# A mixture-of-depths stage in a megakernel: two batches in the row halves, one rank pass, three pairs in flight

## What is computed

```python
h = h + _L2_ffn_ref(_layernorm(h, axis=-1), ...)

def _L2_ffn_ref(x, attention_mask, wr, br, w1, b1, w2, b2):
    k = max(1, int(0.5 * s))
    kk = k - 1 if k > 1 else 1
    weights = (jnp.einsum('bsd,do->bso', x, wr) + br)[..., 0]
    _, idx = jax.lax.top_k(weights, k)
    sel_idx = idx[:, :kk]
    sel = jnp.take_along_axis(x, sel_idx[:, :, None], axis=1)
    hid = jax.nn.gelu(jnp.einsum('bkd,dh->bkh', sel, w1) + b1)
    y = jnp.einsum('bkh,hd->bkd', hid, w2) + b2
    y = y * jnp.take_along_axis(weights, sel_idx, axis=1)[..., None]
    processed = jnp.zeros_like(x).at[batch_idx, sel_idx].set(y)
    return processed + x
```

## Time and profile before

| | |
|---|---|
| median of three runs | 6034.58 us |
| the profiled execution's own time | 5997.16 us |
| its span, first to last instruction | 5995.3 us |
| mean granted TensorE clock over it (1 is 2.4 GHz) | 0.818 |
| busy: TensorE matmul | 5041.0 us (84%) |
| busy: TensorE weight loads | 3453.3 us (58%) |
| busy: VectorE | 3205.9 us (53%) |
| busy: ScalarE | 2330.2 us (39%) |
| busy: GpSimd | 1898.2 us (32%) |

### The profile page before, as it was taken

One profiled execution on the slowest core, in us unless ns is written; L12 is line 12 of the kernel. 1 busy time (PEld: TensorE's weight loads), 2 busy tenths in 40 slices (PEclk: granted clock), 3 DMA queues, 4 the chain that ended last, 5 costly groups with the idle time before them and its releaser, 6 DMA issues. The chain is left out here.

```text
span 5995.3 us, 119454 instructions
## 1 busy us (share of the span) xinstructions
PE 5041.0 (84%) x34045; PEld 3453.3 (58%) x34045; DVE 3205.9 (53%) x9147; ACT 2330.2 (39%) x5857; POOL 1898.2 (32%) x2148
## 2 busy tenths in 40 slices
PE   4419998576677999979997668879999999979999
PEld 4416665355465666656665655545666666646665
DVE  1145553344353466634443446657777777745554
ACT  3313333000011233334442321116777777745555
POOL 0002222111153344422223740004444444433333
PEclk9997776555596699979997555558999999989999
DMA  0010011111121011133331111110000000023332
GB/s 9 7 36 19 21 22 14 33 39 40 39 56 34 19 26 26 25 69 75 81 78 41 42 36 26 27 33 8 10 10 8 10 10 10 9 44 68 75 74 60
DMA packets 522888, 205.69 MB, mean 34 GB/s; under 512 B 491164, under 2 KB 513804, under 8 KB 522636
## 3 DMA queue, kind: packets, MB, share of 16 engines
q1 hardware_dynamic: 522764, 204.15, 15.4%
HBM read 158.15 MB, written 45.91 MB: 34 GB/s over the span
## 5 line engine op out<-in xcount | busy, mean ns | idle before, releaser
L3083 POOL TENSOR_TENSOR att_P<-att_P,att_rden 125x498 f32<-125x498 f32 x512 | 520.8, 1018 | 633.2 <-DVE att_rden L3354 633.2
L3270 ACT ACTIVATE att_P<-att_pS,att_nb 125x249 f32<-125x249 f32 x1024 | 472.7, 476 | 0.3 <-DVE att_nb L3362 0.3
L2474 DVE TENSOR_TENSOR moe_hT<-moe_silu,moe_pH 128x498 f32<-128x498 f32 x384 | 258.9, 674 | 324.3 <-ACT moe_silu L2460 324.3
L3691 ACT ACTIVATE sw_hT<-sw_pH,sw_b 128x498 f32<-128x498 f32 x512 | 318.4, 673 | 242.7 <-PE sw_pH L3645 242.7
L3186 PEld LDWEIGHTS att_pP<-att_ident,att_P 124*125 124x125 f32 (+1 forms) x2048 | 262.5, 187 | 181.0 <-issue 181.0
L3186 PE MATMUL att_pP<-att_ident,att_P 124*125 124x124 f32 (+1 forms) x2048 | 352.5, 294 | 3.8 <-POOL att_P L3083 2.4
L3362 DVE TENSOR_REDUCE att_nb<-att_pS 125x2 f32<-125x498 f32 x512 | 323.0, 668 | 58.1 <-PE att_pS L3174 56.4
L3277 ACT ACTIVATE att_PTr<-att_pP 125x498 f32<-125x498 f32 x512 | 304.9, 596 | 97.7 <-PE att_pP L3186 91.9
L2460 ACT ACTIVATE moe_silu<-moe_pH 128x498 f32<-128x498 f32 x384 | 225.4, 587 | 284.2 <-PE moe_pH L2417 198.4
L1021 PE MATMUL att_pS<-att_kT,att_qT 16*125 16x249 f32 x1024 | 304.7, 482 | 2.1 <-ACT att_kT L1127 1.3
L586 POOL TENSOR_TENSOR att_norm_centered<-att_F,att_norm_sum 125x256 f32<-125x256 f32 (+1 forms) x128 | 85.2, 666 | 662.1 <-DVE att_norm_sum L581 661.8
(11 more groups left out here) (452 smaller groups left out, 12166.2 us busy)
## 6 DMA issues: line engine op xcount, KB each, us to landing
moe_share<-mixing SPq DMA_DIRECT2D x64, 498.0 KB
sw_share<-mixing SPq DMA_DIRECT2D x64, 498.0 KB
att_F<-h_stream SPq DMA_DIRECT2D x192, 62.5 KB
att_X<-h_stream SPq DMA_DIRECT2D x192, 62.5 KB
ffn_w<-in_w1b SPq DMA_DIRECT2D x128, 32.5 KB
ffn_w<-in_L_ffn_W SPq DMA_DIRECT2D x128, 32.0 KB
h_stream<-att_H SPq DMA_DIRECT2D x64, 62.5 KB
ffn_F<-h_stream SPq DMA_DIRECT2D x64, 62.5 KB
```

The costliest lines, as they stand in the source:

```text
L3083: g.tensor_tensor(own, own, bc(rden[:, j % 2, c, :], T), ALU.mult).then_inc(*scaled.one())
L3270: ins = a.activation(P[:, r, c, t, :], pS[:, 2 * r + c, t * T:(t + 1) * T], ACT.Exp, bias=nb[:, r, c, t:t + 1], accum_out=den[:, r, c, t:t ...
L3691: a.activation(hT[:, k % 4, :, :], pH[:, place, :, 0:T], ACT.Relu, bias=b1[:, k:k + 1]).then_inc(*hid_ready.one())
```

## The change

Only `stage_depths2` and its constants change. The new stage is written with `HalfNorm` and `waves`, in three parts (`pre`, `proj`, `main`) of four steps each.

- Both batches of a pair are transposed together, so xT is 128 rows (64 channels of each batch) x 249. Gate and hidden products run once per batch in the row half of that batch (64 rows), the w2 product once per batch and half of the hidden channels onto the column half (64 output rows of pY) of that batch. pY has channels on its rows and is transposed back by two transposes into pT.
- The biases come through ScalarE's bias operand (br for W, b1 for the gelu, b2 for yT) instead of a row of ones.
- A token's own weight comes by four one-row transposes of W on TensorE and a copy of 125x4. The rank of a group is one VectorE instruction: (W - own weight) > tie, summed, where tie is 0 or, for earlier tokens, the negative of the smallest normal number.
- Centering, squares and scaling of the norm move from VectorE and ScalarE to GpSimd, and so do the two closing additions: base = X + xn, and H1 = res + base. The copy to xT moves to ScalarE. VectorE's gate is one instruction.
- SyncE's order is that of `streamed`: F is loaded four pairs ahead, X two pairs ahead, each behind the store in program order.

```diff
+    STEPS, WAVES, ROUNDS = 4, 4, 6
+        norm = HalfNorm(st, bodies=WAVES)
...
+                streamed(sp, ahead, keep, store, 4)
...
             def _(g):
...
+                def pre(n, u, step):
+                    if step == 0:
+                        g.wait_ge(*xn_ready.before(n))
+                        norm.center(g, n, g4(Fi[:, u, :, :, :]))
+                        norm.square(g, n)
+                    if step == 2:
+                        norm.power(g, n)
+                    if step == 3:
+                        if since(n, 2):
+                            g.wait_ge(*xT_done.after(n - 2))
+                            g.wait_ge(*base_ready.after(n - 2))
+                        norm.scale(g, n, g4(xn[:, u, :, :, :])).then_inc(*xn_ready.one())
+                def main(n, u, step):
+                    if step == 1:
+                        g.wait_ge(*kept.after(n, u))
+                        g.wait_ge(*xn_ready.after(n))
+                        g.wait_ge(*h_ready.before(n))
+                        g.tensor_tensor(base[:, :, :], g4(X[:, u, :, :, :]), g4(xn[:, u, :, :, :]), ALU.add).then_inc(
+                            *base_ready.one())
+                    if step == 3:
+                        g.wait_ge(*res_ready.after(n))
+                        g.wait_ge(*base_ready.after(n))
+                        g.wait_ge(*stored.lagging(n, u))
+                        g.tensor_tensor(g4(H1[:, u, :, :, :]), res[:, :, :], base[:, :, :], ALU.add).then_inc(
+                            *h_ready.one())
+                waves(g, (pre, lambda n, u, step: None, main), STEPS)
...
             def _(pe):
...
+                def proj(n, u, step):
                     if step == 0:
+                        pe.wait_ge(*xn_ready.after(n))
+                        pe.wait_ge(*xT_ready.before(n))
+                        for t in range(2):
+                            ins = pe.transpose(pX[:, t * OFF:t * OFF + ROWS[t]],
+                                               xn[0:ROWS[t], u, t, :, :].rearrange("p b c -> p (b c)"),
+                                               ident[0:ROWS[t], 0:ROWS[t]])
+                    if step == 1:
+                        pe.wait_ge(*xT_ready.after(n))
+                        pe.wait_ge(*w_ready.before(n))
+                        pe.wait_ge(*hid_ready.before(n))
                         for b in range(2):
+                            r = slice(b * C, (b + 1) * C)
+                            ins = pe.matmul(pW[:, b, 0:T], wr[r, :], xT[r, :], start=True, stop=True)
+                        ins.then_inc(*w_done.one())
+                        for k in range(2):
+                            for b in range(2):
+                                r = slice(b * C, (b + 1) * C)
+                                ins = pe.matmul(pH[:, b, k * T:(k + 1) * T], w1[r, k * 128:(k + 1) * 128], xT[r, :],
+                                                start=True, stop=True)
+                def main(n, u, step):
+                    if step == 0:
+                        pe.wait_ge(*w_ready.after(n))
+                        pe.wait_ge(*n_ready.before(n))
+                        for t in range(2):
+                            for b in range(2):
+                                g = 2 * t + b
+                                ins = pe.transpose(pN[:, g:g + 1], W[0:1, u, b, t * OFF:t * OFF + PT],
+                                                   ident[0:1, 0:1])
+                    if step == 1:
+                        pe.wait_ge(*hid_ready.after(n))
+                        pe.wait_ge(*yT_ready.before(n))
+                        for k in range(2):
+                            for b in range(2):
+                                ins = pe.matmul(pY[b * C:(b + 1) * C, 0:T], w2[:, k, :], hT[:, u, k, b, :],
+                                                start=(k == 0), stop=(k == 1))
+                    if step == 2:
+                        pe.wait_ge(*yT_ready.after(n))
+                        pe.wait_ge(*res_ready.before(n))
+                        for t in range(2):
+                            ins = pe.transpose(pT[:, t * 128:(t + 1) * 128], yT[:, t * OFF:t * OFF + PT], ident[:, :])
...
             def _(a):
+                def proj(n, u, step):
+                    if step == 0:
+                        a.wait_ge(*xT_done.after(n))
+                        a.wait_ge(*hid_done.before(n))
+                        a.activation(xT[:, :], pX[:, 0:T], ACT.Copy).then_inc(*xT_ready.one())
+                    if step == 1:
+                        a.wait_ge(*w_done.after(n))
+                        a.activation(W[:, u, :, :], pW[:, :, 0:T], ACT.Identity, bias=br[:, 0:1]).then_inc(
+                            *w_ready.one())
+                        a.wait_ge(*hid_done.after(n))
+                        for k in range(2):
+                            ins = a.activation(hT[:, u, k, :, :], pH[:, :, k * T:(k + 1) * T], ACT.Gelu_apprx_tanh,
+                                               bias=b1[:, k:k + 1])
+                def main(n, u, step):
+                    if step == 1:
+                        a.wait_ge(*y_done.after(n))
+                        a.wait_ge(*turned.before(n))
+                        a.activation(yT[:, :], pY[:, 0:T], ACT.Identity, bias=b2[:, 0:1]).then_inc(*yT_ready.one())
...
             def _(v):
+                def pre(n, u, step):
                     if step == 0:
+                        v.wait_ge(*loaded.after(n, u))
+                        norm.sums(v, n, g4(Fi[:, u, :, :, :]))
+                    if step == 2:
+                        norm.spread(v, n, 1e-5)
+                def main(n, u, step):
+                    if step == 0:
+                        v.wait_ge(*n_done.after(n))
+                        v.wait_ge(*gate_ready.before(n))
+                        v.tensor_copy(wn[:, :, :].rearrange("p t b -> p (t b)"), pN[:, 0:4]).then_inc(*n_ready.one())
+                    if step == 1:
+                        for t in range(2):
+                            for b in range(2):
+                                v.scalar_tensor_tensor(out=junk[:, b, :], in0=W[:, u, b, :], scalar=wn[:, t, b:b + 1],
+                                                       in1=ties[:, t, :], op0=ALU.subtract, op1=ALU.is_gt,
+                                                       accum_out=count[:, t, b:b + 1]).then_inc(*counted.one())
+                    if step == 3:
+                        v.scalar_tensor_tensor(gate[:, :], count[:, :, :].rearrange("p t b -> p (t b)"), float(KEEP),
+                                               wn[:, :, :].rearrange("p t b -> p (t b)"), ALU.is_lt,
+                                               ALU.mult).then_inc(*gate_ready.one())
+                        v.wait_ge(*gate_ready.after(n))
+                        v.wait_ge(*turned.after(n))
+                        v.wait_ge(*h_ready.before(n))
+                        v.tensor_tensor(res[:, :, :], pT[:, 0:256].rearrange("p (g c) -> p g c", g=4),
+                                        bc(gate[:, :], C), ALU.mult).then_inc(*res_ready.one())
```

More of the change, by code:

```diff
@@ L105 @@
     "mod2.stored": 2,
-    "mod2.vec": 16,
     "moe1.const_loaded": 6,
@@ new lines, in _, with ahead, keep @@
+                const(sp, cl, b2[:, :], A["mod2_b2"])
+                const(sp, cl, br[:, :], every_row(A["mod2_br"], PT))
+                const(sp, cl, ties[:, :, :], A["const_order"])
+                def ahead(n, u):
+                    sp.wait_ge(*norm.centered.lagging(n))
+                    st.held(sp)
+                    for ins in load_pair(sp, Fi[:, u, :, :, :], h, n):
+                        ins.then_inc(*loaded.one(u))
+                def keep(n, u):
+                    sp.wait_ge(*base_ready.lagging(n))
+                    st.held(sp)
+                    for ins in load_pair(sp, X[:, u, :, :, :], h, n):
+                        ins.then_inc(*kept.one(u))
@@ L2856, in _, with store @@
+                def store(n, u):
+                    sp.wait_ge(*h_ready.after(n))
+                    st.held(sp)
+                    for ins in store_pair(sp, h, H1[:, u, :, :, :], n):
+                        ins.then_inc(*stored.one(u))
+                streamed(sp, ahead, keep, store, 4)
+                for n in (PAIRS - 2, PAIRS - 1):
+                    sp.wait_ge(*stored.after(n, n % 2))
             @block.gpsimd
             def _(g):
-                g.wait_ge(*f.memset_done.after(0))
@@ L2860, in front @@
[L2860 to L2865, removed]
+                g.wait_ge(*memset_done.after(0))
+                def pre(n, u, step):
[10 more added lines that the diff above has]
+                        norm.scale(g, n, g4(xn[:, u, :, :, :])).then_inc(*xn_ready.one())
@@ L2867, in _ @@
+                waves(g, (pre, lambda n, u, step: None, main), STEPS)
             @block.tensor
             def _(pe):
-                pe.wait_ge(*f.const_loaded.after(0))
-                pe.wait_ge(*f.memset_done.after(0))
```

(5 more changed lines are left out.)

182 lines of the change are left out of this document (80 added, 102 removed).

## The result

The changed kernel takes 5775.04 us (median of 4 runs, 5756.35 to 5806.98), the kernel before, run beside it on the same chip, 6029.09 (4 runs, 5962.52 to 6040.81). The ratio is 0.9625, 95% interval 0.9582 to 0.9668: faster. The forecast was 5795, range 5745 to 5850. The profiled execution of after has a span of 5805.2 us, that of before 5995.3.

The account below looks back on a forecast made before the run. TensorE at 1.2 GHz bounds the old stage; then a ring across engines does: 13.5 + 31 x 6.9 = 227 us for 469.2, plus 1 for constants. 6034.6 - 241 = 5793, said as 5795, range 5745 to 5850.

Parts of the forecast that it names:

- The bound of before: Old mod2 stage: TensorE at 1.2 GHz in one chain, 14.66 us a pair; VectorE's rank work lies beside it.
- The ring: New stage: GpSimd scaling, TensorE products, VectorE product, GpSimd's last addition, next scaling; 5.5 us at 2.4 GHz, 8.3 at 1.2.
- The clock: TensorE in the new stage: half the pairs at either level, mean clock about 0.75, 6.9 us a pair.
- high clock: Rival: TensorE in the new stage stays at 2.4 GHz nearly always, stage 180 to 192 us, time 5747 to 5760; chance 0.23.
- VectorE's term: VectorE's work in the new stage: 4.2 us a pair, 2.1 of it four counts, fitting inside the turn.
- GpSimd's additions: Two closing additions of 125x256 moved to GpSimd in the new stage, taken as 0.66 us each, 1.32 together.
- Table loads: Rival: ScalarE loads two tables a pair, switching between Identity with bias and gelu; +16 us, time 5811; chance 0.04.
- The halves: Rival: TensorE's half-array passes don't overlap, 0.21 us each instead of 0.13; ring near 9.3, time about 5870; chance 0.03.
- No overlap: Rival: X loads late for GpSimd's first addition, pairs run one after another; 15.4 us a pair, time 6059; chance 0.03.
- carrying the distance between profile and median over: Whole kernel: the runs' median stood 37 us above the profiled execution before, and was taken to do so again.

Follow-up runs that it names:

- e1: Kernel before with only the one-pass rank (four subtract-and-compare passes for eight comparisons and an addition): stage 468.5 us against 469.2, ratio 0.998.
- e2: Changed kernel with GpSimd's scaling moved ahead of its last addition, right behind the power: stage 201.9 us against 242.4, ratio to before 0.9586.
- e3: Changed kernel with three added dense TensorE products a pair, result unused: stage 201.4 us against 242.4, ratio to before 0.9524.
- e6: Changed kernel with early scaling, the square on ScalarE ahead of the gelu and two unused dense products a pair: stage 185.0 us, ratio to before 0.9544.
- e7: Changed kernel with its four rank counts done twice: stage 246.3 us against 242.4, ratio to before 0.9606.
- e4: Changed kernel with the norm's square moved from GpSimd to ScalarE in step 1, behind the gelu: stage 327.6 us against 242.4, ratio to before 0.9766.
- e5: Changed kernel with the norm's square moved from GpSimd to ScalarE in step 0, ahead of the gelu: stage 242.4 us, ratio to before 0.9622.
- e9: e6 without its two dense products a pair: stage 201.9 us against 185.0, ratio to before 0.9577.
- e10: Changed kernel with both passes of one array half in a row (hidden, w2) and three unused dense products a pair: stage 198.8 us, one execution 5737.56 us.

## Why the prediction was right, point by point

**The bound of before** was right: removing 66 us of VectorE work alone gave 0.7 (e1).

**The ring** was right in every link and releaser that the turn shown has, and e2 shows that it set the time. Step by step at the turn shown, start to start: crossing and scaling 0.76 (0.24 + 0.61 taken: 0.85), transposes 0.58, w2 1.86, gate product 0.94, hidden 0.93, closing transposes and crossing 0.58, product and crossing 0.68, last addition 0.69; sum 7.02. The forecast's two sums at the same steps, mixed as the clock was in this turn (transposes, w2 and gate at 1.2 GHz, the rest at 2.4), give 0.85 + 0.61 + 1.98 + 0.98 + 1.04 + 0.43 + 0.1 + 0.42 + 0.08 + 0.66 = 7.15. Small errors of opposite sign lie in it: the crossing from VectorE to GpSimd was 0.26, not 0.08 (3712.12 + 0.42 to 3712.80), the one from GpSimd to TensorE 0.15, not 0.24, and the w2 and hidden passes were 0.1 shorter each than taken.

**The clock** was the disputed step. Half the pairs at either level was written, clock 0.75. Measured: 0.68, and no turn of after is at 2.4 GHz throughout. In four of six both levels lie inside the turn, which comes to nearly the same sum (7.0 against 6.9), and that is luck, since the prediction had whole turns at either level. In the other two (clock 0.53 and 0.63, against 0.76 in the four) w2, gate and hidden passes are all at 1.2 GHz, and they take 8.2 and 7.9, against 8.3 in the sum for that level. They make the mean 7.3 and account for most of the stage's excess: 242.4 against 227. With the clock held high the stage takes 201 (e3, with its added products); the rival *high clock* had 180 to 192.

**VectorE's term was mis-sized** and it did not matter. Four counts were taken at 0.53 with their read-out, 2.1 together; groups by shape of after:
```profile
L3043 DVE SCALAR_TENSOR_TENSOR mod_junk<-mod_W,mod_wn,mod_ties 125x249 f32<-125x249 f32 x128 | 101.3, 844 | 0.1
...
L2915 POOL TENSOR_TENSOR mod_base<-mod_X,mod_xn 125x256 f32<-125x256 f32 x32 | 28.4, 888 | 0.2 <-POOL mod_H L2922 0.2
L2922 POOL TENSOR_TENSOR mod_H<-mod_res,mod_base 125x256 f32<-125x256 f32 x31 | 22.7, 732 | 58.1 <-DVE mod_res L3055 58.1
...
L3006 ACT ACT_TABLE_LOAD x1 | 1.3, 1283 | 0.0
```
They took 844 ns each on the mean; the 480 came from a stage in which GpSimd was busy only 32 of 469 us. So the turn of VectorE is 5.3 us, not 4.2 (7.02 less its wait of 1.68). GpSimd's additions took 0.89 and 0.73 for 0.66, which had been scaled from another shape; attention 1 of the kernel before has one of the very shape (L1868), at 0.72. At a turn of 5.5 this closes a second ring, as e3 and e6 show; at 7.0 VectorE had 1.7 us of slack (e7). The *high clock* rival was thereby priced too low, as far as e3 with its added products can tell.
The Trainium skill (page "SBUF — State Buffer", section "Who interferes with whom") says that a VectorE instruction with two inputs in SBUF contends with a GpSimd instruction that reads SBUF, and one with a single input, outside the two-port modes, does not. The trace agrees: counts 0.81 to 0.93 against 0.47, while a reduction, with its one input, takes 0.41 beside GpSimd's addition (3712.67 in after) and 0.42 in the earlier trace rows. It would have been the rule to weigh.

**Table loads** did not come: one load of 1283 ns in the stage, as in the earlier trace rows. **The halves** overlap as in the earlier trace rows: eight passes in 1.00, at 2.4 GHz, their starts in pairs 0.004 us apart. The price of 0.21 for a pass that does not overlap stands in no row above; the trace of before has it, the full passes behind 1741.82 starting 0.210 apart. **No overlap** did not come: GpSimd's first addition waited 0.2 us in all. e4 shows a turn partly in series, norm and products in line: 10.1 us, where the rival had 15.4 for all of it.

**The whole time** was right to 0.35% (5775 for 5795), with two errors of opposite sign, so the closeness is luck. The stage took 15 us more than forecast; the runs of after came out lower than the profiled execution of before had let expect (the profile of after, at 5807, is the slowest of its four runs, where I had put the median 37 us above the profiled one). That step, carrying the distance between profile and median over, was a guess about scatter of unchanged stages and should have widened the range, not moved its middle. The medians differ by 254 us and the stage by 227; the 27 between them are not shown to be the change's work.

## What to carry to other kernels

When a change makes a bound engine cheap, write down the ring that closes through the program order of all engines, with each link at both levels of the clock, and look for a short instruction that stands in it only by order: moving one such scaling was worth 40 us. Moving work to an idle engine is worth nothing off the ring (e5) and costs 85 us if it lands behind something late (e4). Judge a stage by its own span where other stages scatter by more than the effect. Price an instruction from a row in which the engines beside it do what they will do in the new stage.

## What the runs showed of the chip that I had not expected

- A VectorE operation with two operands of 125x249 in SBUF takes 0.47 us alone and 0.81 to 0.93 beside GpSimd operations on whole tiles; GpSimd's addition of two full tiles takes 0.89 beside it, 31 times of 32 in after, and 0.73 beside a reduction.
- Waits of 1.65 us of TensorE in a turn were followed by passes at 1.2 GHz (w2 1.93), with a stage clock of 0.68; with the wait filled down to 0.5 to 1.1 by dense products it is 0.95. Three added dense products a pair shortened the stage by 41 us in e3, two by 17 in e6 against e9.
- Products of 64 rows take 1.0 to 1.1 us for eight passes of 249 columns at 2.4 GHz whether the halves alternate (1.01, e3) or not (1.11, e10): two run in the 0.21 us of one full-array pass in either order.
